# Second message layer of a graph network: the sums table kept turned, fp32 messages as weights, and a last node stage of half-height products

## The reference

```python
h = relu(layernorm(x))                       # 50000 x 64
msgs = relu(concat(h[dst], h[src]) @ mW1 + mb1) @ mW2 + mb2      # one row for each edge
agg = segment_sum(msgs, dst, 50000)          # sums table: 50000 x 64
out = relu(concat(h, agg) @ uW1 + ub1) @ uW2 + ub2
x = x + out                                  # the result
```

## Time and profile before

| what | value |
| --- | --- |
| median of 3 runs | 2256.64 us (2255.74 to 2258.77) |
| the profiled execution: span from its first to its last instruction | 2674.4 us |
| mean granted share of TensorE's full clock in it | 0.684 |
| busy share of the span: PE, DVE, ACT, POOL | 66%, 59%, 32%, 60% |
| edge layer 0 in it (268 to 1345 us) | 1077 us |
| edge layer 1 in it (1499 to 2448 us) | 949 us |
| last node stage in it (2448 us to the end) | 227 us |

### The profile page before, as it was taken

The page is one execution under the profiler, slowest core; times in us unless marked ns, Lnnn a source line. Parts: engine busy times, 40 slices in busy tenths (PEclk is TensorE's granted clock), DMA queues, the critical chain, the costliest instruction groups (busy, mean ns, idle before and its releaser), DMA issues. The chain is left out here.

```text
span 2674.4 us, 57997 instructions
## 1 busy us (share of the span) xinstructions
PE 1766.8 (66%) x16123; PEld 1480.6 (55%) x16123; DVE 1570.1 (59%) x5935; ACT 855.7 (32%) x3189; POOL 1598.2 (60%) x1364
## 2 busy tenths in 40 slices
PE   3764666665666666666700277678677777668998
PEld 2544656665666656666600266567566666556554
DVE  6884656666666666566649445455544545546554
ACT  3772323232323223232327321112111212113665
POOL 5884888888888888888876544344443444430332
PEclk9885555555555555555555678788787978888999
DMA  3774554444555445554337532223222323222665
GB/s 123 238 243 134 108 88 91 89 89 82 91 90 88 90 82 91 91 91 87 59 64 245 159 80 69 60 69 77 68 60 68 78 64 76 67 59 56 187 187 150
DMA packets 342556, 273.14 MB, mean 102 GB/s; under 512 B 144824, under 2 KB 273504, under 8 KB 342474
## 3 DMA queue, kind: packets, MB, share of 16 engines
q1 hardware_dynamic: 259028, 233.22, 30.0%
q0 software_dynamic: 81536, 38.61, 13.5%
q10 hardware_dynamic: 1910, 0.37, 0.1%
HBM read 206.69 MB, written 65.34 MB: 102 GB/s over the span
## 5 line engine op out<-in xcount | busy, mean ns | idle before, releaser
L1261 POOL DMA_INDIRECT x<-e_sums,e_to x392 | 628.2, 1603 | 146.1 <-issue 112.4
L907 POOL DMA_INDIRECT e_near_source<-h,e_near_ids x392 | 387.4, 988 | 528.4 <-PE bank L1027 215.4
L1498 PE MATMUL bank<-e_window,e_onehot 128*128 128x64 f32 x2352 | 527.0, 423 | 159.9 <-DVE e_onehot L1286 128.5
L1498 PEld LDWEIGHTS bank<-e_window,e_onehot 128*128 128x128 f32 x2352 | 509.1, 331 | 180.0 <-issue 121.4
L1061 PE MATMUL bank<-e_near_parts,e_near_to_node 128*128 128x64 bf16 x4704 | 216.4, 198 | 203.8 <-issue 199.7
L1236 POOL DMA_INDIRECT e_ends<-wh,e_ids x296 | 289.3, 977 | 101.2 <-issue 100.3
L1017 PE MATMUL bank<-e_near_to_edge,e_near_window 128*64 128x128 f32 x2352 | 220.8, 335 | 183.6 <-DMA e_near_window<-h 148.8
L1546 PE MATMUL bank<-e_parts,e_same 128*128 128x64 bf16 x2940 | 177.5, 241 | 233.2 <-DVE e_parts L1355 134.2
L1061 PEld LDWEIGHTS bank<-e_near_parts,e_near_to_node 128*128 128x128 bf16 x4704 | 181.4, 101 | 247.9 <-issue 229.3
L1546 PEld LDWEIGHTS bank<-e_parts,e_same 128*128 128x128 bf16 x2940 | 166.6, 131 | 250.8 <-issue 250.7
L990 ACT ACTIVATE e_near_hid<-bank,mb_col 128x512 f32<-128x512 f32 x98 | 67.4, 688 | 724.5 <-PE bank L1037 494.6
(11 more groups left out here) (175 smaller groups left out, 3303.6 us busy)
## 6 DMA issues: line engine op xcount, KB each, us to landing
e_window<-wh SPq DMA_DIRECT2D x392, 96.0 KB
e_near_window<-h SPq DMA_DIRECT2D x392, 96.0 KB
e_owners<-ends SPq DMA_DIRECT2D x98, 256.0 KB
n_x<-x SPq DMA_DIRECT2D x98, 256.0 KB, 3.2
n_x<-in_x_dram SPq DMA_DIRECT2D x49, 256.0 KB
wh<-n_wh SPq DMA_DIRECT2D x49, 256.0 KB
x<-n_x SPq DMA_DIRECT2D x49, 256.0 KB
e_rel<-rel SPq DMA_DIRECT2D x98, 128.0 KB
```

What stands on the lines that cost most here:

```text
L907: pool.indirect_dma_start(out=t.source[s][:, j, :], out_offset=None, in_=tabs["h1"], in_offset=bass.IndirectOffsetOnAxis(ap=t.ids[s][:, j: ...
L1261: pool.indirect_dma_start(out=added_tab, out_offset=bass.IndirectOffsetOnAxis(ap=t.to[s][:, j:j + 1], axis=0), in_=t.sums[s][:, j, :], in_ ...
L1498: last = nc.tensor.matmul(bank[FIND_BANKS[s]][:, j * D:(j + 1) * D], onehot, window, start=w == 0, stop=w == WK - 1)
```

## The change

The sums table is kept turned. Features lie on the partitions and nodes along the free axis: partition 64 (n mod 2) + feature, column n div 2, so that two neighbouring nodes share a column. Its size is the same.

In the near form the messages stay fp32, and the three parts with their two casts and two subtractions go away. The messages are now the weights (128 edges x 64 features), and an fp32 one-hot of 194 columns is streamed against them, once for the even nodes (into partitions 0 to 63) and once for the odd ones (64 to 127): 8 products of 194 columns for a group instead of 48 of 64. DVE's add takes 194 columns instead of 256. `msgs` has two buffers, and the bias now waits for the sums of two groups before.

In the last node stage the table needs no turning. `h` is loaded with two neighbouring rows beside each other, so that 4 turns give it the same layout as the table; a copy of the table's 512 columns replaces the copy beside `h`. The first product is split by what it multiplies: 4 products with 64 partitions each (even and odd nodes, `h` and sums), two added up in each of two PSUM banks. Loads and stores of this stage are in pieces of 512 bytes (two rows). The relu writes straight through, without reordering.

`prepare` loads `uW1` as four half matrices (13 small loads instead of 10), and works out one scaled place less. The form that is not taken with these inputs gets a turning stage of its own.

```diff
-AB = 4
-SPAN = AB * P
-LAST_AT = NB - AB
+COLS = NB * P // 2
+HALF = WINDOW // 2 + 2
+LAST_AT = COLS - HALF
...
-    c["agg"] = sb("agg_sb", [P, NB * D])
+    c["agg"] = sb("agg_sb", [P, COLS])
...
-            nc.vector.tensor_scalar(t.to_node[s % 2][:, j, :], c["in_span"][:],
+            nc.vector.tensor_scalar(t.to_node[s % 2][:, j], c["in_span"][:],
...
     def bias(s, k):
         dve.wait_ge(t.mlp_done, count(s, k, 0, ESLOTS))
+        if has(s, k, 2, ESLOTS):
+            dve.wait_ge(t.summed, 2 * count(s, k, 2, ESLOTS))
...
-        here = c["agg"][:, bass.ds(places[s][j], AB * D)]
-        sums = bank[4 + 2 * (s % 2) + j // 2][:, j % 2 * AB * D:(j % 2 + 1) * AB * D]
+        here = c["agg"][:, bass.ds(places[s][j], HALF)]
+        sums = bank[4 + 2 * (s % 2) + j // 2][:, j % 2 * HALF:(j % 2 + 1) * HALF]
         nc.vector.tensor_tensor(here, sums, here, ALU.add).then_inc(t.agg_ready, 1)
...
-                           (-10, of(add, 2)), (-8, leave), (-10, of(add, 3)), (-8, of(to_node, 2)), (0, ids), (-8, low),
+                           (-10, of(add, 2)), (-8, of(to_node, 2)), (-10, of(add, 3)), (0, ids),
...
-    rounds_of_blocks(act, [(-6, relu), (-8, high), (-4, copy_ends), (-8, mid)], ESLOTS, GROUPS)
+    rounds_of_blocks(act, [(-6, relu), (-4, copy_ends)], ESLOTS, GROUPS)
...
     def sums(s, k):
         pe.wait_ge(t.to_node_ready, G * count(s, k, 0, ESLOTS))
-        pe.wait_ge(t.high_ready, count(s, k, 0, ESLOTS))
-        pe.wait_ge(t.mid_ready, count(s, k, 0, ESLOTS))
-        pe.wait_ge(t.low_ready, count(s, k, 0, ESLOTS))
+        pe.wait_ge(t.msgs_ready, count(s, k, 0, ESLOTS))
...
-            for b in range(AB):
-                at = (j % 2 * AB + b) * D
-                for part in range(3):
-                    last = nc.tensor.matmul(to[:, at:at + D], t.to_node[s % 2][:, j, b * P:(b + 1) * P],
-                                            t.parts[s % 2][:, part, j, :], start=part == 0, stop=part == 2)
+            for odd in range(2):
+                last = nc.tensor.matmul(to[odd * D:(odd + 1) * D, j % 2 * HALF:(j % 2 + 1) * HALF], t.msgs[s % 2][:, j, :],
+                                        t.to_node[s % 2][:, j, odd, :], start=True, stop=True)
...
+        def pairs(tab, base, q):
+            return tab[bass.ds(base, q * 2 * P), :].rearrange("(q p i) d -> p q (i d)", q=q, i=2)
...
-                sp.dma_start(hs[s][:, :, 0, :], tabs["h1"][bass.ds((k * SLOTS + s) * BLOCK, BLOCK), :]
-                             .rearrange("(r p) d -> p r d", p=P)).then_inc(h1_in[s], 16)
+                sp.dma_start(h[s][:], pairs(tabs["h1"], (k * SLOTS + s) * BLOCK, Q)).then_inc(h1_in[s], 16)
...
-            rounds_of_blocks(dve, [(-4, copy_outT), (0, beside), (-1, high), (-4, result)])
+            rounds_of_blocks(dve, [(-4, copy_outT), (0, beside), (-4, result)])
...
             def first(s, k):
+                pe.wait_ge(hT_ready, count(s, k))
                 pe.wait_ge(beside_ready, count(s, k))
-                for i in range(2):
-                    last = nc.tensor.matmul(hid_bank[s % 2][i][:], c["uw1"][:], hsT[s % 2][:, i * H:(i + 1) * H],
-                                            start=True, stop=True)
+                for weights, of in ((c["uw1_h"], hT[s % 2]), (c["uw1_agg"], aggT[s % 4])):
+                    for i in range(2):
+                        half = slice(i * D, (i + 1) * D)
+                        last = nc.tensor.matmul(hid_bank[s % 2][i][:], weights[half, :], of[half, :],
+                                                start=weights is c["uw1_h"], stop=weights is c["uw1_agg"])
```

More of the change, by code:

```diff
@@ L30 @@
 NB = 392
[L31 to L33 removed]
+COLS = NB * P // 2
+HALF = WINDOW // 2 + 2
+LAST_AT = COLS - HALF
+TURNS = COLS // P
 AHEAD = ESLOTS - 1
@@ L842, in edge_vectors, with apart, keep_turned @@
 def edge_vectors(nc, dve, c, near, far, layer):
-    both_ways(c, dve, lambda: edge_vector(nc, dve, c, near, layer, True) if layer == 0 else near_vector(nc, dve, c, near),
-              lambda: edge_vector(nc, dve, c, far, layer, False))
+    def apart():
+        edge_vector(nc, dve, c, far, layer, False)
+        def keep_turned(s, k):
+            dve.wait_ge(far.rows_turned, count(s, k, 0, ESLOTS))
+            nc.vector.tensor_copy(c["agg"][:, bass.ds((ESLOTS * k + s) * P, P)], c["bank"][s % 2][:, 0:P]
+                                  ).then_inc(far.rows_kept, 1)
+        if layer == 1:
+            rounds_of_blocks(dve, [(0, keep_turned)], ESLOTS, TURNS)
+    both_ways(c, dve, lambda: edge_vector(nc, dve, c, near, layer, True) if layer == 0 else near_vector(nc, dve, c, near), apart)
 def edge_scalars(nc, act, c, near, far, layer):
@@ L852, in edge_tensors, with apart, turn_sums @@
 def edge_tensors(nc, pe, c, near, far, layer):
-    both_ways(c, pe, lambda: edge_tensor(nc, pe, c, near, layer, True) if layer == 0 else near_tensor(nc, pe, c, near),
-              lambda: edge_tensor(nc, pe, c, far, layer, False))
+    def apart():
+        edge_tensor(nc, pe, c, far, layer, False)
+        def turn_sums(s, k):
+            pe.wait_ge(far.rows_in[s], 16 * (k + 1))
+            if has(s, k, 2, ESLOTS):
+                pe.wait_ge(far.rows_kept, count(s, k, 2, ESLOTS))
+            nc.tensor.transpose(c["bank"][s % 2][:, 0:P], far.rows[s][:], c["ident"][:]).then_inc(far.rows_turned, 1)
+        if layer == 1:
+            rounds_of_blocks(pe, [(0, turn_sums)], ESLOTS, TURNS)
+    both_ways(c, pe, lambda: edge_tensor(nc, pe, c, near, layer, True) if layer == 0 else near_tensor(nc, pe, c, near), apart)
 class NearBuffers:
@@ L1728, in flip @@
                     pe.wait_ge(res_ready, count(s, k, 1))
-                for q in range(R // 2):
+                for q in range(Q):
                     last = nc.tensor.transpose(bank[7][:, q * P:(q + 1) * P], outT[s % 2][:, q * P:(q + 1) * P],
```

139 lines of the change are left out of this document (59 added, 80 removed).

## The result

The change makes the kernel slower by 0.29%: 2264.57 us (median of 11 runs, 2260.64 to 2269.67) against 2257.04 for the kernel before (11 runs beside them, 2255.53 to 2260.77); the ratio is 1.0029, its 95% interval 1.0021 to 1.0038. That is just above the 0.2% that a measurement can tell from no change. The prediction was 2241 us, faster with a chance of 0.64. The time lies in the range, 2195 to 2265, but the sign is wrong.

A forecast was written before the change was run, and what follows sets the result against it. It took POOL to bound edge layer 0, PE with POOL right behind edge layer 1, and PE the last stage. Terms -16 - 3 + 4 = -15 us gave 2249 from 2264, or 2241 from the median; range 2195 to 2265.

The forecast's parts named there:

- The base: Whole kernel: profiled span of 2674 us less 410 us of TensorE stops gives 2264 us, near the timed median of 2257.
- The stops: Edge layer 1: TensorE's 226 us of waits with no releaser in the profile, taken as the profiler's own, absent when timed.
- rival (c): Edge layer 1: TensorE's stops are real in timed runs and partly go with fewer records; 2080 to 2215 us, chance 0.11.
- PE's group falls to 4.85 us: Edge layer 1: TensorE's time per group falls from 5.25 us as the sums shrink to 1.3; range 4.8 to 6.1.
- What is late next: POOL, 5.09 us: Edge layer 1: gathers set the pace, 5.00 to 5.21 us a group, 5.09 taken against 5.25; -16 us.
- rival (a): Edge layer 1: POOL already sets the pace or ties, so mostly no change; 2250 to 2262 us, chance 0.20.
- The term of -16: Edge layer 1: 98 groups going from 5.25 to 5.09 us at POOL's pace, bounds -4 to -39 us.
- End of the layer: Edge layer 1's last six steps: no gather left, so TensorE's 0.4 us a group counts, partly behind DVE; -3 us.
- The last stage: Last node stage: halved turn worth 0, first product unchanged, change of shape 0.08 us a block; +4 us (0 to +8).
- Second to flip: Last node stage: time from second product to flip stays 1.87 us, since flip waits for DVE's copy; halved turn worth 0.
- rival (b): Last node stage: first's half products run one after the other, 3.4 instead of 1.7 us; about 2322 us, chance 0.13.
- Sum: Whole kernel: -16 for edge layer 1's pace, -3 for its end, +4 for the last stage; -15 us in all.

## Why the prediction was wrong

- **The base: right.** The stops were not in the timed runs, and the sum without them (2264 from the span) was 5 us from the second profile's 2259. But neither the reason I gave for them, the profiler, nor rival (c)'s, PE's many records, is borne out: the unchanged kernel has no stops in its second profile, with as many records. What stopped PE in that one execution stays open.
- **"PE's group falls to 4.85 us": failed, 5.16.** The sums to find came out as predicted (1.20 for 1.3). But I re-priced the sums alone, and put the border ahead of them at nothing: the change of shape, which cost 0.05 us at most behind the bf16 sums, costs 0.31 in front of the fp32 ones. Taken from hidden to find the step goes from 0.43 + 1.71 = 2.14 to 0.74 + 1.20 = 1.94, a gain of 0.20 instead of 0.41, and find to turn gave 0.11 of it back, for a reason that no run shows. I had a change of shape as a term in the last stage, but not here.
- **"What is late next: POOL, 5.09 us": failed; the engine was right, the size decided the sign.** The measured pace was 5.29, outside my 5.00 to 5.21. I took gathers from a profile in which DVE's 478 us of work were spread over 949. In the second profile the same work fills 536 us, and the gathers meet more of it: between 1560 and 1980 us, 301 of 321 run beside a one-hot, 89 of 173 in the first. So they take 1008 ns before already, a tie with PE. That is rival (a), which had the tie but priced it at -4 us and expected no longer gathers. Its terms add up to 2254 to 2258 us, not 2250 to 2262; either lies below the measured time. And the change adds to DVE's one-hots what stretches them to 1028 ns. I costed the longer one-hots as DVE's own time, "worth nothing by itself"; their price was POOL's. The term of -16 became +5.7 us.
- **End of the layer:** -3 predicted, -1.8 measured.
- **The last stage: mechanism right, size off, and that the total (+1.4 for +4) is near is luck.** Second to flip stayed at 1.87, halves ran side by side (rival (b) fell), the DMA pieces stayed hidden. The change of shape cost 0.19 us a block, not 0.08, and more than the 0.15 that I took as its bound from second to turn: +8.9 for +4. The rule of the Trainium skill, "TensorEngine Tiling (Array Packing)", Key Properties, that such a change drains TensorE, agrees with it, and with the 0.31 in the edge layer, which I hadn't put it to; the 0.05 behind the bf16 sums doesn't show it. Two gains that I had not looked for took most of it back. At the start, by the rows of the two traces, a block needs four turns instead of eight, while PE's loads still take twice their later time (eight in 1.57 us, later 0.86): -2.9 us. At the end, the last store, -4.6: the 50,000 rows leave 848 for the last block, and the kernel before stored them as 106 pieces of 2 KB. Its transfers, from 2252.5 to 2258.5 us in 40 slices (share of the 16 engines in tenths):

```profile
DMA  0011102001210111011120111200111111111100
```

and the changed kernel's last rows, two stores in pieces of 512 bytes, from 2262.2 to 2263.2 us:

```profile
DMA  0000356999999999999999999999998310000000
```

The Trainium skill, "DMA: Bandwidth & Descriptors", section "Why a DMA increments its semaphore by 16 and not by 1", says that a transfer is spread over the largest number of engines up to 16 that divides the slowest dimension of both its sides; 106 has 2 as the largest such divisor. The share of a tenth or so before, 2 of 16, agrees. The length of the pieces alone isn't the cause: the store ahead of it, 256 KB from 128 partitions in the same pieces of 2 KB, moved in 0.8 us (2250.3 to 2251.1).

- **Sum:** predicted -16 - 3 + 4 = -15; in the traces +5.7 - 1.8 + 1.4 = +5.3, with the -0.5 ahead of the layer +4.8. The timed difference, 7.5 us, has some 3 us more. The two profiled executions differ by 2265.72 - 2260.99 = 4.7 us in their own times, and the interval, 0.21% to 0.38%, begins at 4.7, so the rest can lie in the spread of the runs.

## What to carry to other kernels

A span far above the timed runs calls for a second profile before any duration is read from it: not only the total is wrong, but an operation that contends with another one can look cheaper there, as the gathers did (988 ns, then 1008). Where two engines tie, ask of each edit what it does to the other engine's operations, not only to its own queue. And a step between two starts contains whatever lies at its border: when a step gets a new shape, it is to be priced together with the changes of shape that it makes ahead of it and behind it.

## What the runs showed that I had not expected

- A change of the shape of PE's weights costs 0.19 us from 128 to 64 partitions (0.59 for 0.40 us), and 0.31 from 128 to 64 columns (0.74 for 0.43), at a granted clock of 0.98 and 0.99. The same four 128-column products of message, cut into eight of 64 columns, went from 0.88 to 0.57 us (2014.29 - 2013.72).
- DVE's fp32 one-hots lengthen GpSimd's indirect gathers, and those that ACT makes don't: 1025 ns a gather with all on DVE, 998 with half of the sums' on ACT, 1001 with half of their columns left out.
- The last store of 106 partitions took 6 us for 212 KB; the same rows in pieces of 512 bytes less than 1 us, and a store of 256 KB from 128 partitions 0.8 us.
